# A transformer block on one core: attention products by groups of 512 queries, probabilities in contiguous blocks, one query buffer

## The chip, the core and the metric

The kernel runs on one core of a Trainium2 chip. The core has TensorE (matrix products, in profiles PE; its weight loads are PEld), VectorE (DVE), ScalarE (ACT), GpSimd (POOL) and SyncE (SP, which here only issues transfers). Each engine runs its own instructions in order and waits on semaphores. The metric is device time in microseconds (us) for one execution.

## What is computed

One layer: multi-head attention over 1024 tokens with 16 heads (128 plain and 64 rotary dimensions), a small side attention over tokens chosen by a gate, an output projection with residual and normalization, and a ternary-weight gated MLP with another normalization. The part that the change is about, from the reference:

```python
q = jnp.concatenate([q_nope, q_pe], axis=-1)
k = jnp.concatenate([k_nope, k_pe], axis=-1)
scores = jnp.einsum('bhqd,bhkd->bhqk', q, k) * scale
scores = jnp.where(causal[None, None], -jnp.inf, scores)
probs = jax.nn.softmax(scores.astype(jnp.float32), axis=-1).astype(q.dtype)
attn = jnp.einsum('bhqk,bhkd->bhqd', probs, v)
...
x = _layernorm(x + _L0_attn_ref(x, ...), axis=-1)
x = _layernorm(x + _L0_ffn_ref(x, ...), axis=-1)
```

## The kernel before

**Number format.** Nearly every operand of a product is kept as two parts, a high part (name ends in h) and a low part (l). ScalarE writes the high part as a copy, VectorE the low part as a subtraction (both by one helper line each, L1140 and L1298), and `three` (L838) makes three products: high by high, high by low, low by high.

**Tiles.** The 1024 queries of a head lie in 8 tiles of 128. For tile i: `qk` makes the scores against 128(i+1) keys on TensorE, into one of two buffers SC; VectorE masks them and finds the row extreme (L1367); ScalarE takes the exponential into Pb (`exp`, L1157); TensorE transposes Pb by 128x128 pieces (`tc`, L873), up to four into one of the ring's four buffers J0 to J3; ScalarE and VectorE bring them to PTh and PTl. Then `pv` multiplies the values Vh, Vl with PTh, PTl for a group of queries, the result goes to ATh, ATl, and `wo` multiplies it with the head's output weights and VectorE adds it to acc: a reciprocal (L1555) and two additions (L1563) per 256 queries.

**Groups before.** A `pv` group is 256 queries, two tiles; group g needs the keys of 2g+2 tiles, so a head has groups of 2, 4, 6 and 8 key tiles. PTh is `[128, 8 key tiles, 256]`, ATh has two buffers of 256. Each head parity has its own query buffer QNh, QNl, written in halves of 512 by `qn`.

**Order.** The order of everything is written out by hand in `head_steps`: a head has 8 slots, slot i begins with `qk` of tile i, then come two other steps, then `exp` of tile i (the place after which it comes is exp_at), then the rest. Each engine goes through this one list and runs its own part of each step, so a step that is placed later on TensorE is placed later on ScalarE and VectorE too. A ring step takes the next of J0 to J3 and waits until the step four places back in the ring has been read out. Steps next to the change: `kvn2` (four normalizations on ScalarE, L1252), `kt` (transposed keys), `ab` (head weights, which read Wqnh, Wqnl), `qp`, `kv`, `kpe` (projections for the next two heads), and, in the last two heads, `tern` (ternary weights), `rowadd`, `ln1` (row statistics, L1500 and L1504), `ln1n` (normalization, L1509), `ht` (transposes of the result for the MLP), `ug` (up and gate products of one of 32 MLP steps, 0 to 31), `m` (its activation) and `dn`.

**Passes.** Heads run in pairs, an even head and an odd one. The first pair is written out (FIRST), pairs 1 to 6 are a hardware loop (MID), the last pair is LAST, and EPILOGUE ends head 15 and runs the MLP.

## Time and profile before

| | |
|---|---|
| median of 3 runs | 686.48 us (684.96 to 688.63) |
| profiled execution | 685.76 us, its span 683.9 us |
| mean granted TensorE clock | 0.992 of full |
| TensorE busy | 645.7 us of the span |
| weight loads busy | 582.5 us |
| VectorE busy | 474.8 us |
| ScalarE busy | 400.3 us |
| GpSimd busy | 371.9 us |

Products are pipelined: each row of the timeline has the length of one product, but the next one starts long before it ends, so the distance between two starts says what it costs. Times in rows are counted from the start of the span. "idle before" is time in which the engine had nothing running, with what ended it.

### The profile page before, as it was taken

The numbers are of one execution on the slowest core, as the hardware profiler recorded it, in microseconds if no ns is written. First come the engines' busy times: TensorE is split into PE (matmuls) and PEld (weight loads), VectorE is DVE, ScalarE is ACT, GpSimd is POOL, SyncE is SP. The second block draws the span as 40 slices with busy tenths as digits, with TensorE's granted clock in tenths as the row PEclk, the third lists the DMA queues.
The fourth block names the chain that finished last, engine by engine and source line by source line (L and its number), as shares of the span: only waits on it lengthen the run. The fifth ranks groups of instructions, "written<-read, shape, count | busy, mean of one in ns | idle before, by whom it ended". The sixth has DMA issues, their size and how long they took to land.

```text
span 683.9 us, 14087 instructions
## 1 busy us (share of the span) xinstructions
PE 645.7 (94%) x4456; PEld 582.5 (85%) x4456; DVE 474.8 (69%) x1291; ACT 400.3 (59%) x934; POOL 371.9 (54%) x331
## 2 busy tenths in 40 slices
PE   8899989999999999999999999999999999889895
PEld 5788987898889988898889888988899888779895
DVE  4877367565766667666856586658666667897996
ACT  4884346744764475646664757456744767445552
POOL 7873368463844473456627472738454715431564
PEclk9999999999999999999999999999999999999998
DMA  7307142410451046103610342114510482000001
GB/s 233 115 2 176 41 93 50 114 56 16 109 132 54 0 99 154 54 0 92 146 46 23 92 101 60 54 46 92 115 54 0 108 240 75 10 1 1 1 17 47
DMA packets 23551, 49.85 MB, mean 73 GB/s; under 512 B 3168, under 2 KB 16352, under 8 KB 21600
## 3 DMA queue, kind: packets, MB, share of 16 engines
q1 hardware_dynamic: 22144, 47.82, 27.3%
q10 hardware_dynamic: 1376, 1.64, 0.7%
q8 instruction: 17, 0.28, 0.2%
q14 instruction: 14, 0.11, 0.1%
HBM read 16.94 MB, written 1.05 MB: 26 GB/s over the span
## 4 chain that ended last, share of the span: by engine, by line
PE 55%; DVE 14%; ACT 13%; issue 11%; POOL 4%; DMA 1%; DVEq 0%; ACTq 0%; POOLq 0%; SPq 0%
PE J L840 9%; PE J L842 9%; PE J L841 9%; PE J L873 4%; ACT Pb L1157 4%; DVE PTl L1298 4%; ACT kvraw L1252 3%; PE SC L860 3%; DVE SC L1367 3%; PE SC L862 3%; PE SC L861 3%; PE SC L864 3%; PE SC L863 3%; POOL rstd L711 3%; ACT PTh L1140 2%
## 5 line engine op out<-in xcount | busy, mean ns | idle before, releaser
L1298 DVE TENSOR_TENSOR PTl<-J,PTh 128x512 fp32r<-128x512 f32 (+1 forms) x192 | 102.8, 553 | 67.4 <-ACT PTh L1140 66.4
L1157 ACT ACTIVATE Pb<-SC,nm 128x128 f32<-128x128 f32 (+7 forms) x128 | 94.9, 741 | 54.8 <-DVE nm L1367 54.3
L1367 DVE CUSTOM_DVE_ANT_0 SC<-SC,mask 128x128 f32<-128x128 f32 (+7 forms) x128 | 97.1, 759 | 21.2 <-PE SC L864 20.0
L873 PE MATMUL J<-ident,Pb 128*128 128x128 f32 x576 | 88.9, 280 | 6.4 <-ACT Pb L1157 5.1
L840 PE MATMUL J<-PTh,Vh 128*128 128x256 f32 x320 | 88.7, 277 | 6.4 <-DVE PTl L1298 6.3
L1140 ACT ACTIVATE PTh<-J 128x512 fp32r<-128x512 f32 (+1 forms) x192 | 88.1, 492 | 8.3 <-PE J L873 7.6
L841 PE MATMUL J<-PTl,Vh 128*128 128x256 f32 x320 | 89.5, 280 | 0.0
L842 PE MATMUL J<-PTh,Vl 128*128 128x256 f32 x320 | 89.5, 280 | 0.0
L873 PEld LDWEIGHTS J<-ident,Pb 128*128 128x128 f32 x576 | 64.3, 141 | 15.4 <-ACT Pb L1157 6.8
L840 PEld LDWEIGHTS J<-PTh,Vh 128*128 128x128 f32 x320 | 60.2, 188 | 13.9 <-DVE PTl L1298 12.8
L860 PE MATMUL SC<-KNh,QNh 128*128 128x128 f32 (+2 forms) x192 | 69.3, 361 | 0.1
L1140 ACT ACTIVATE ATh<-J 128x256 fp32r<-128x256 f32 x64 | 24.5, 382 | 74.8 <-PE J L842 74.1
L862 PE MATMUL SC<-KNh,QNl 128*128 128x128 f32 (+2 forms) x192 | 66.0, 344 | 0.0
L863 PE MATMUL SC<-KK,QS 128*128 128x128 f32 (+2 forms) x192 | 66.0, 344 | 0.0
L861 PE MATMUL SC<-KNl,QNh 128*128 128x128 f32 (+2 forms) x192 | 65.9, 343 | 0.0
L864 PE MATMUL SC<-KK,QS 128*128 128x128 f32 (+2 forms) x192 | 65.9, 343 | 0.0
L1298 DVE TENSOR_TENSOR ATl<-J,ATh 128x256 fp32r<-128x256 f32 x64 | 27.0, 422 | 49.5 <-ACT ATh L1140 49.3
L841 PEld LDWEIGHTS J<-PTl,Vh 128*128 128x128 f32 x320 | 60.3, 188 | 0.4
L842 PEld LDWEIGHTS J<-PTh,Vl 128*128 128x128 f32 x320 | 60.5, 189 | 0.0
L1563 DVE SCALAR_TENSOR_TENSOR acc<-J,rs,acc 128x256 f32<-128x256 f32 x128 | 56.1, 480 | 2.7
L1252 ACT ACTIVATE kvraw<-kvraw,nmr,rstd 128x128 f32<-128x128 f32 x128 | 52.6, 486 | 2.5 <-POOL nmr L821 2.5
L1140 ACT ACTIVATE kvraw<-J 128x512 f32<-128x512 f32 x32 | 19.1, 598 | 58.1 <-PE J L842 58.1
(305 smaller groups left out, 1886.5 us busy)
## 6 DMA issues: line engine op xcount, KB each, us to landing
KK<-RK SPq DMA_DIRECT2D x30, 512.0 KB, 6.3
QS<-RQh SPq DMA_DIRECT2D x15, 256.0 KB, 7.5
QS<-RQl SPq DMA_DIRECT2D x15, 256.0 KB, 6.5
KX<-KX SPq DMA_DIRECT2D x14, 256.0 KB, 2.3
QX<-QX SPq DMA_DIRECT2D x14, 256.0 KB, 2.4
r_kv<-in_W_ckv SPq DMA_DIRECT2D x7, 384.0 KB, 3.5
r_o<-in_W_o SPq DMA_DIRECT2D x18, 128.0 KB, 2.1
r_qn<-in_W_qT SPq DMA_DIRECT2D x16, 128.0 KB, 2.1
```

Of the source, the lines that this page charges most:

```text
L840: mm(o, lhsT=wh, rhs=xh, start=start, stop=False)
L841: mm(o, lhsT=wh, rhs=xl, start=False, stop=False)
L842: return mm(o, lhsT=wl, rhs=xh, start=False, stop=stop)
L860: mm(o[:, k], lhsT=QNh[b][:, q], rhs=KNh[b][:, k], start=True, stop=False)
L861: mm(o[:, k], lhsT=QNh[b][:, q], rhs=KNl[b][:, k], start=False, stop=False)
L862: mm(o[:, k], lhsT=QNl[b][:, q], rhs=KNh[b][:, k], start=False, stop=False)
L863: mm(o[:, k], lhsT=QS[b][:, q], rhs=KD[b][:, k], start=False, stop=False)
L873: last = pe.transpose(o[:, tile(j - 4 * c)], Pb[i % 2][:, tile(j)], ident[:, :])
L1140: return act.activation(o, i, ACT.Copy)
L1157: act.activation(Pb[i % 2][:, w], SC[i % 2][:, s], ACT.Exp, bias=nm[:, i % 2:i % 2 + 1], scale=-1.0, accum_out=sm[:, b, i:i + 1]).then_inc ...
L1298: dve.tensor_tensor(o, i, h.bitcast(F32), ALU.subtract).then_inc(done[kind], 1)
L1367: dve.tensor_tensor_reduce(out=SC[i % 2][:, s], in0=SC[i % 2][:, s], in1=mask[:, 128 * (7 - i):S], scale=-SCALE, scalar=HIGH, op0=ALU.add, ...
```

## The change

Groups of 512 queries, two per head. Group g takes the key tiles below it (group 1: four, each with all 512 queries as one row), and four key tiles on its diagonal, with 512, 384, 256 and 128 queries. PTh and PTl become 29 blocks of 128 columns, laid out so that each of these rows is contiguous; `key_blocks` says to which blocks the transposes of a tile go. The blocks of group 0's diagonal lie where group 1's first keys lie. ATh and ATl are one buffer of 512 each. QNh and QNl are one buffer for all heads: half c is rewritten once tile 4c+3 of the head before has been scored. Wqnh and Wqnl move into a gap of PTh and PTl.

```diff
+DIAG = [0, 16]
+GAP = 26
+BLOCKS = 29
+def key_blocks(n):
+    i = TILE_OF[n]
+    g, ii, full = i // 4, i % 4, i >= 4 and n == CH0[i]
+    first, step, nb = (ii, 4, 4) if full else (DIAG[g] + ii, 3, ii + 1)
+    return slice(first, first + step * (nb - 1) + 1, step), nb
...
-        QNh.append(sb("QNh1", [128, S], F32R))
+        QNh.append(QNh[0])
...
-        PTh, PTl = sb("PTh", [128, T, 256], F32R), sb("PTl", [128, T, 256], F32R)
-        ATh = [sb(f"ATh{i}", [128, 256], F32R) for i in range(2)]
+        PTh, PTl = sb("PTh", [128, BLOCKS * 128], F32R), sb("PTl", [128, BLOCKS * 128], F32R)
+        ATh, ATl = sb("ATh", [128, 512], F32R), sb("ATl", [128, 512], F32R)
+        Wqnh, Wqnl = [X[:, 128 * GAP:128 * GAP + 256].rearrange("p (r n) -> p r n", r=2) for X in (PTh, PTl)]
...
+                add(6, True, ("ln1", 0, 0), ("ln1", 0, 1))
+                add(7, True, ("ln1n", 0, 0), *t(h, 6), ("ht", 0, 0), ("ln1n", 0, 1))
...
-            exp_at = [[2, 2, 2, 2, 2, 2, 2, 2], [2, 2, 2, 2, 2, 2, 2, 2]]
+            exp_at = [[2, 2, 2, 2, 2, 2, 2, 1], [2, 2, 2, 2, 2, 2, 2, 1]]
...
+                if i % 4 == 0 and not first:
+                    pe.wait_ge(done["qn"], count("qn", h, i // 4))
                 if i == 0 and not first:
-                    pe.wait_ge(done["qn"], count("qn", h, 1))
...
-                pe.wait_ge(pt_lo, NCH * h + CH0[2 * g + 2])
-                for j in range(2 * g + 2):
-                    q = slice(0, 256) if j <= 2 * g else slice(128, 256)
-                    last = three(o[:, q], Vh[b][:, j, :], Vl[b][:, j, :], PTh[:, j, q], PTl[:, j, q], j == 0, j == 2 * g + 1)
+                if g == 1:
+                    pe.wait_ge(pt_lo, NCH * h + CH0[7] + 1)
+                    for j in range(4):
+                        q = slice(512 * j, 512 * j + 512)
+                        three(o[:, :], Vh[b][:, j, :], Vl[b][:, j, :], PTh[:, q], PTl[:, q], j == 0, False)
+                pe.wait_ge(pt_lo, NCH * h + CH0[4 * g + 4])
+                for r in range(4):
+                    j, q = 4 * g + r, slice(128 * (DIAG[g] + 4 * r), 128 * (DIAG[g] + 3 * r + 4))
+                    last = three(o[:, 128 * r:], Vh[b][:, j, :], Vl[b][:, j, :], PTh[:, q], PTl[:, q], j == 0, r == 3)
...
-                    pe.wait_ge(done["pv"], count("pv", u, c))
+                    pe.wait_ge(done["pv"], count("pv", u, c // 2))
...
                     if kind == "qn":
+                        if not (isinstance(u, int) and u == 0):
+                            hold(act, sc_ready, T * (u - 1) + 4 * c + 4)
...
-                        wait(act, ready["wo"], 4 * u + c - 1)
-                        copy(ATh[c % 2][:, :], o[:, 0:256]).then_inc(hi["pv"], 1)
+                        wait(act, ready["wo"], 4 * u + 2 * c)
+                        copy(ATh[:, :], o[:, :]).then_inc(hi["pv"], 1)
```

The step lists change with it. In the loop, group 0 of a head stands in slot 5, right behind `qk` 5; group 1 stands in slot 1 of the next head. Steps wo 2 and wo 3 of a head are both in slot 2 of the next one. Steps wo 0 and wo 1 of the even head are in its slot 6; of the odd head, wo 0 is in slot 7 and wo 1 in slot 0 of the next head. The second half of `qn` is in slot 7, and `exp` of tile 7 comes after one step instead of two. In slot 2 of the even head the order is now tc of tile 1, kt 0, wo 2, kt 1, wo 3.

TensorE at the first product group of a head in the loop, before (J2 is a buffer of the ring, PTh and PTl the transposed probabilities, Vh0 and Vl0 the values of the even head), in the even head: the group of two key tiles, in slot 3.

```order
L840 MATMUL J2<-PTh,Vh0 128x256
L841 MATMUL J2<-PTl,Vh0 128x256
L842 MATMUL J2<-PTh,Vl0 128x256
L840 MATMUL J2<-PTh,Vh0 128x128
L841 MATMUL J2<-PTl,Vh0 128x128
L842 MATMUL J2<-PTh,Vl0 128x128
```

And after, the first group of the even head, in slot 5.

```order
L847 MATMUL J2<-PTh,Vh0 128x512
L848 MATMUL J2<-PTl,Vh0 128x512
L849 MATMUL J2<-PTh,Vl0 128x512
L847 MATMUL J2<-PTh,Vh0 128x384
L848 MATMUL J2<-PTl,Vh0 128x384
L849 MATMUL J2<-PTh,Vl0 128x384
L847 MATMUL J2<-PTh,Vh0 128x256
L848 MATMUL J2<-PTl,Vh0 128x256
L849 MATMUL J2<-PTh,Vl0 128x256
L847 MATMUL J2<-PTh,Vh0 128x128
L848 MATMUL J2<-PTl,Vh0 128x128
L849 MATMUL J2<-PTh,Vl0 128x128
```

Sixty products of a head, in four groups, become 36 in two.

VectorE in slots 6 and 7 of the last head, before: from the mask of tile 6 (128x896) to that of tile 7 (128x1024).

```order
L1367 ISA SC0,nm<-SC0,mask 128x896
L1367 ISA nm 128x1
L1298 TENSOR_TENSOR PTl<-J0,PTh 128x4x128
L1298 TENSOR_TENSOR PTl<-J1,PTh 128x2x128
L1555 RECIPROCAL rs<-sm 128x2
L1563 SCALAR_TENSOR_TENSOR acc<-J2,rs,acc 128x256 x2
L1517 TENSOR_TENSOR QS0<-J3,QNh0 128x256
L1517 TENSOR_TENSOR KK0<-J3,QNl0 128x256
L1500 BN_STATS st<-acc 128x6 x2
L1504 BN_AGGR mvl<-st 128x2 x2
L1367 ISA SC1,nm<-SC1,mask 128x1024
```

The same stretch after.

```order
L1380 ISA SC0,nm<-SC0,mask 128x896
L1380 ISA nm 128x1
L1311 TENSOR_TENSOR PTl<-J1,PTh 128x4x128
L1311 TENSOR_TENSOR PTl<-J2,PTh 128x2x128
L1566 RECIPROCAL rs<-sm 128x2
L1574 SCALAR_TENSOR_TENSOR acc<-J3,rs,acc 128x256 x2
L1566 RECIPROCAL rs<-sm 128x2
L1574 SCALAR_TENSOR_TENSOR acc<-J0,rs,acc 128x256 x2
L1511 BN_STATS st<-acc 128x6 x2
L1515 BN_AGGR mvl<-st 128x2 x2
L1511 BN_STATS st<-acc 128x6 x2
L1515 BN_AGGR mvl<-st 128x2 x2
```

The mask of tile 7 follows. A second wo and the first row statistics have come ahead of it; the low part of ht 0 has gone behind it.

TensorE between the transposes of tile 6 and of tile 7 in the last head, before, is filled by two up/gate steps of eight products each (the first of them shown) and a wo.

```order
L873 MATMUL J1<-ident,Pb0 128x128 x4
L873 MATMUL J2<-ident,Pb0 128x128 x3
L1053 MATMUL SC0<-QNh0,xTh 128x256
L1054 MATMUL SC0<-QS0,xTh 128x256
L1053 MATMUL SC0<-QNl0,xTh 128x256
```

After, only the transposes of ht 0 (L1030) lie between them, and the up/gate steps follow ht 1.

```order
L881 MATMUL J1<-ident,Pb0 128x128 x4
L881 MATMUL J2<-ident,Pb0 128x128 x3
L1030 MATMUL J3<-ident,acc 128x128 x4
L881 MATMUL J0<-ident,Pb1 128x128 x4
L881 MATMUL J1<-ident,Pb1 128x128 x4
L1030 MATMUL J2<-ident,acc 128x128 x4
L1066 MATMUL SC0<-QNh0,xTh 128x256
```

The last product group stands behind two of these up/gate steps; before, it stood behind four.

## Rows read from the trace of the kernel before

**Rows 1.** The page, part 1: busy us, share of the span, instructions.

```profile
PE 645.7 (94%) x4456; PEld 582.5 (85%) x4456; DVE 474.8 (69%) x1291; ACT 400.3 (59%) x934; POOL 371.9 (54%) x331
```

**Rows 2.** Busy time by stretch: stretch, its length, engines, clock, DMA.

```profile
core 0: us, PE busy (x) PEld busy (x) DVE busy (x) ACT busy (x) POOL busy (x), PEclk, DMA share, GB/s
200.00:280.00 80.00, 78.21 (x533) 70.40 (x534) 52.94 (x145) 50.35 (x120) 43.22 (x32) 1.00 0.27 66
600.00:683.90 83.90, 71.47 (x565) 68.81 (x564) 70.39 (x178) 40.99 (x100) 34.75 (x53) 0.97 0.04 14
```

**Rows 3.** Who TensorE waited for from 120 to 520: total, times, longest.

```profile
PE J L840 <- DVE PTl L1298: 3.1, 15, 0.3
PE J L873 <- ACT Pb L1157: 2.4, 11, 0.3
PE J L989 <- ACT kvraw L1252: 2.4, 5, 0.5
```

**Rows 4.** TensorE's timeline: start, length, line, tiles, shape.

```profile
300.65 0.28 PE L840 MATMUL J<-PTh,Vh 128*128 128x256 f32 x1
...
302.42 0.22 PE L840 MATMUL J<-PTh,Vh 128*128 128x128 f32 x1
...
302.71 0.95 PE L873 MATMUL J<-ident,Pb 128*128 128x128 f32 x7
...
318.31 0.34 PE L861 MATMUL SC<-KNl,QNh 128*128 128x384 f32 x1
...
318.84 0.33 PE L864 MATMUL SC<-KK,QS 128*128 128x384 f32 x1
...
329.08 0.39 PE L841 MATMUL J<-qcl,ABh 128*128 128x512 f32 x1
...
329.77 0.39 PE L1005 MATMUL J<-qcs,ABl 128*128 128x512 f32 x1
```

**Rows 5.** TensorE's timeline: waits in one pass, and the next pass's first.

```profile
304.44 1.09 PE L873 MATMUL J<-ident,Pb 128*128 128x128 f32 x8 [0.28 <-ACT Pb L1157]
...
317.67 0.63 PE L989 MATMUL J<-ident,kvraw 128*128 128x128 f32 x4 [0.47 <-ACT kvraw L1252]
...
376.87 0.33 PE L873 MATMUL J<-ident,Pb 128*128 128x128 f32 x1 [0.28 <-ACT Pb L1157]
```

**Rows 6.** Timeline of ScalarE and TensorE in slot 2 of an even head.

```profile
343.93 0.39 ACT L1140 ACTIVATE ATh<-J 128x256 fp32r<-128x256 f32 x1 [2.23 <-PE J L842]
...
344.82 1.65 ACT L1252 ACTIVATE kvraw<-kvraw,nmr,rstd 128x128 f32<-128x128 f32 x4
...
344.99 0.44 PE L873 MATMUL J<-ident,Pb 128*128 128x128 f32 x2 [0.17 <-ACT Pb L1157]
```

**Rows 7.** VectorE: two groups of the page's part 5, then one subtraction.

```profile
L1298 DVE TENSOR_TENSOR ATl<-J,ATh 128x256 fp32r<-128x256 f32 x64 | 27.0, 422 | 49.5 <-ACT ATh L1140 49.3
L1563 DVE SCALAR_TENSOR_TENSOR acc<-J,rs,acc 128x256 f32<-128x256 f32 x128 | 56.1, 480 | 2.7
...
620.99 0.69 DVE L1298 TENSOR_TENSOR PTl<-J,PTh 128x512 fp32r<-128x512 f32 x1 [0.25 <-ACT PTh L1140]
```

**Rows 8.** Timeline of the last head: VectorE's masks, statistics and normalization.

```profile
604.94 0.69 DVE L1367 CUSTOM_DVE_ANT_0 SC<-SC,mask 128x512 f32<-128x512 f32 x1
...
617.98 0.75 DVE L1500 BATCH_NORM_STATS2 st<-acc 128x6 f32<-128x256 f32 x2
...
618.92 1.23 DVE L1367 CUSTOM_DVE_ANT_0 SC<-SC,mask 128x1024 f32<-128x1024 f32 x1
...
622.94 0.73 DVE L1509 TENSOR_SCALAR acc<-acc,mvl,rsd 128x256 f32<-128x256 f32 x2
```

**Rows 9.** TensorE: the last product with V, and up/gate step 9.

```profile
628.96 0.27 PE L842 MATMUL J<-PTh,Vl 128*128 128x128 f32 x1
...
639.89 0.39 PE L1053 MATMUL SC<-QNh,xTh 128*128 128x256 f32 x1 [0.74 <-DVE CS L1462]
```

**Rows 10.** One stretch with its granted clock (columns as in rows 2).

```profile
570.00:575.00 5.00, 5.00 (x25) 4.83 (x24) 3.71 (x13) 3.50 (x8) 2.39 (x2) 0.67 0.50 171
```

More of the change, by code:

```diff
@@ L181, in attention_and_mlp @@
         Pb = [sb(f"Pb{i}", [128, S]) for i in range(2)]
-        PTh, PTl = sb("PTh", [128, T, 256], F32R), sb("PTl", [128, T, 256], F32R)
-        ATh = [sb(f"ATh{i}", [128, 256], F32R) for i in range(2)]
-        ATl = [sb(f"ATl{i}", [128, 256], F32R) for i in range(2)]
+        PTh, PTl = sb("PTh", [128, BLOCKS * 128], F32R), sb("PTl", [128, BLOCKS * 128], F32R)
+        ATh, ATl = sb("ATh", [128, 512], F32R), sb("ATl", [128, 512], F32R)
+        Wqnh, Wqnl = [X[:, 128 * GAP:128 * GAP + 256].rearrange("p (r n) -> p r n", r=2) for X in (PTh, PTl)]
         wip = KX[:, :, :]
@@ L289, in attention_and_mlp @@
         PER = {"xs": 4, "qc": T, "qm": 4, "kv": 4, "kpe": 2, "qp": 2, "qps": 2, "kt": 2, "ab": 1, "qn": 2,
-               "vs": 1, "pv": 4, "wo": 4, "side": 13, "tc": NCH, "wb": 1, "rwt": 1, "wtot": 3, "ht": 2}
+               "vs": 1, "pv": 2, "wo": 4, "side": 13, "tc": NCH, "wb": 1, "rwt": 1, "wtot": 3, "ht": 2}
         def count(kind, unit, c):
@@ L314, in attention_and_mlp @@
             ("qk", 0, 3), ("qn", 0, 1), ("rqrows", 0, 1), ("kt", 0, 1), ("exp", 0, 3), ("rkrows", 0, 0), ("rkrows", 0, 1),
[L315 removed]
+            ("ab", 1, 0), *t(0, 2), ("kvn2", 0, 2), ("vsh", 0, 1), ("wkv", 1, 0),
             ("qk", 0, 4), ("exp", 0, 4), ("top8", 0, 0), *t(0, 3), ("stk", 1, 0), ("stq", 1, 0), ("kvn2", 0, 3), ("vs", 1, 0),
[L317 to L318 removed]
+            ("qn", 1, 0), ("top8", 0, 1), ("kt", 1, 0), ("top8", 0, 2),
+            ("qk", 0, 5), ("pv", 0, 0), ("exp", 0, 5), ("top8", 0, 3), *t(0, 4), ("kt", 1, 1),
             ("qk", 0, 6), ("side", 0, 2), ("exp", 0, 6), *t(0, 5), ("wosp", 2, 0), ("wqn", 2, 0), ("wqp", 1, 0), ("kv", 1, 0),
             ("side", 0, 3), ("side", 0, 4), ("wo", 0, 0), ("wo", 0, 1),
[L321 removed]
+            ("qk", 0, 7), ("side", 0, 5), ("exp", 0, 7), ("kv", 1, 1), ("side", 0, 6), ("qn", 1, 1), ("kpe", 1, 0), ("kpe", 1, 1),
             ("ropek", 1, 0), *t(0, 6), ("side", 0, 7), ("kv", 1, 2), ("side", 0, 8), ("kv", 1, 3), ("side", 0, 9)]
@@ L418, in head_steps @@
                 add(4, first, ("io", 1, 0))
-                add(6, more, ("qn", n, 1))
                 add(4, more and not first, ("io", 1, 0))
-                add(6, True, *t(h, 5), ("wo", h, 1))
+                add(6, True, *t(h, 5))
+                add(6, last, ("wo", h, 0), ("wo", h, 1))
                 add(5, more, ("rw", n, 0))
                 add(6, more, ("skip", 0, 0))
-                add(7, more, ("wosp", h + 2, 0), ("wqn", h + 2, 0))
-                add(7, True, ("pv", h, 2), *t(h, 6))
+                add(7, more, ("wo", h, 0), ("qn", n, 1), ("wosp", h + 2, 0), ("wqn", h + 2, 0))
+                add(7, not last, *t(h, 6))
             if last:
@@ L470, in mlp_steps_of @@
             return a
-        EPILOGUE = [("wo", NH - 1, 2), *t(NH - 1, 7), one("ug", 2), one("ht", 1), one("m", 0), one("ug", 3), ("pv", NH - 1, 3),
-                    one("m", 1), one("ln1", 2), one("ug", 4), one("m", 2), ("wo", NH - 1, 3), one("ln1n", 2), one("ug", 5),
-                    one("m", 3), one("ln1", 3), one("ug", 6), one("m", 4), one("ln1n", 3)]
+        EPILOGUE = [*t(NH - 1, 7), one("ht", 1), one("ug", 0), one("ug", 1), one("m", 0), ("pv", NH - 1, 1), one("m", 1),
+                    one("ug", 2), one("ug", 3), ("wo", NH - 1, 2), one("m", 2), ("wo", NH - 1, 3), one("ug", 4), one("ln1", 2),
+                    one("m", 3), one("ug", 5), one("ln1n", 2), one("ln1", 3), one("ug", 6), one("m", 4), one("ln1n", 3)]
         for n in range(7, NM):
@@ L1023, in use @@
                 if kind == "wo":
-                    pe.wait_ge(done["pv"], count("pv", u, c))
+                    pe.wait_ge(done["pv"], count("pv", u, c // 2))
                     for t in range(2):
-                        last = three(o[:, 256 * t:256 * t + 256], ATh[c % 2][:, tile(t)], ATl[c % 2][:, tile(t)],
+                        q = tile(2 * (c % 2) + t)
+                        last = three(o[:, 256 * t:256 * t + 256], ATh[:, q], ATl[:, q],
                                      ABh[b][:, 256:512], ABl[b][:, 256:512], True, True)
@@ L1164, in run @@
                     if kind == "tc":
-                        i = TILE_OF[c]
-                        k = 4 * (c - CH0[i])
-                        nb = min(4, i + 1 - k)
-                        copy(PTh[:, k:k + nb, tile(i % 2)],
+                        blocks, nb = key_blocks(c)
+                        copy(PTh[:, :].rearrange("p (j q) -> p j q", q=128)[:, blocks, :],
                              o[:, 0:128 * nb].rearrange("p (j q) -> p j q", j=nb)).then_inc(hi["tc"], 1)
@@ L1370, in run @@
                     if kind == "tc":
-                        i = TILE_OF[c]
-                        k = 4 * (c - CH0[i])
-                        nb = min(4, i + 1 - k)
-                        dst = (slice(None), slice(k, k + nb), tile(i % 2))
-                        lo("tc", u, c, PTl[dst], o[:, 0:128 * nb].rearrange("p (j q) -> p j q", j=nb), PTh[dst])
+                        blocks, nb = key_blocks(c)
+                        h_, l_ = [X[:, :].rearrange("p (j q) -> p j q", q=128)[:, blocks, :] for X in (PTh, PTl)]
+                        lo("tc", u, c, l_, o[:, 0:128 * nb].rearrange("p (j q) -> p j q", j=nb), h_)
                     if kind == "xs":
```

42 lines of the change are left out of this document (16 added, 26 removed).

## The prediction

> **What bounds the kernel now.** I read the page's busy shares first. TensorE is busy 645.7 us of 683.9 [rows 1]. The stages then show where it is not: in the loop it is busy 78.2 of every 80 us, while VectorE has 53; from 600 us on TensorE has 71.5 of 83.9 and VectorE 70.4 [rows 2]. So the loop is bound by TensorE's own work, and the end is shared with VectorE. The waits in the loop agree: three kinds, 7.9 us in 400, none over 0.5 us [rows 3]. One pass (two heads) takes 376.87 - 304.44 = 72.43 us [rows 5]. Work taken from TensorE in the loop is time; a wait there is time too. In the last head and behind it, what counts is also when VectorE gets to an operation, for it runs in order.
>
> **The products with V.** What a product costs is the distance to the next start, not its length. From 300.65 to 302.42 lie 15 products of 256 columns: 0.118 us each. The three of 128 columns behind them take 0.29 together. The 512-wide rows lie 0.230 apart (0.69 for three), the 384-wide ones 0.177 [rows 4]. Before, a head has 48 products of 256 columns and four triples of 128: 48 x 0.118 + 4 x 0.29 = 6.82 us. After: 18 of 512, 6 of 384, 6 of 256 and two triples: 4.14 + 1.06 + 0.71 + 0.58 = 6.49. That is 0.33 a head, 5.3 us over 16 heads, of which 0.66 in a pass. The columns streamed are the same; only starts are saved. I take the measured distances for PTh too. Should the 512-wide ones lie 2 x 0.118 = 0.236 apart, the saving is 0. That is the lower bound.
>
> The page "TensorE: Matmul & The Clock Gate" of the Trainium skill (section "Wait — 56ns, not 53.3ns?") puts start-to-start at columns / 2.4 GHz plus about 2.5 ns. By it the 384 starts saved would be worth 384 x 2.5 ns = 0.96 us, an estimate from that page. The rows have 6 ns for two joined halves where that rule has 2.5, and the row decides.
>
> **Copies of the product.** The split of a group's result goes from 4 x 256 to 2 x 512 columns. VectorE's 256-wide subtraction is 422 ns, its 512-wide one 0.69 us [rows 7]: 4 x 0.42 - 2 x 0.69 = 0.3 us a head less there, and as little on ScalarE. VectorE has 27 us in 80 free in the loop [rows 2], so this is nothing there. The copy to the blocks has the same 128-element runs as before; only the stride between them changes: nothing.
>
> **Waits in the loop.** Three places move.
> First, the exponential of tile 7 now stands ahead of ScalarE's next copy instead of behind the copy of a product group. The wait at 304.44, 0.28 [rows 5], goes. But the new query copy (qn) sits behind it, its low part is needed before the ring's buffer is free, and the transposes of tile 7 wait for that some 0.4: even.
> Second, in slot 2 of the even head. The second group is 15 x 0.230 + 3 x 0.177 + 3 x 0.118 + 0.29 = 4.63 us instead of 21 x 0.118 + 0.29 = 2.77, its copy on ScalarE 0.2 longer than the 256-wide one, and the exponential of tile 1 stands behind it. So the wait at 344.99, 0.17, becomes 0.4. Behind that exponential stand four normalizations, 1.65 us [rows 6], then the copy of tile 1's transposes, which must be through before wo 3 gets buffer 1: another 0.25. Together +0.45.
> Third, in the odd head the wait of 0.47 at 317.67 [rows 5] for the same normalizations. Now TensorE has 1.8 us more of products ahead of it, so this place loses about 0.5.
> The sum is about 0; one run of transposes fewer between products gives 0.1, and rounding of the stretches another 0.05. So -0.83 a pass, -5.0 over six. Bounds: 0 (all new waits real, none of the old gone: +0.8 a pass) to -9 (all 1.4 us of waits gone by half).
>
> The single query buffer costs nothing: half 0 is written when tile 3 of the head before is long scored, half 1 behind qk 7 in TensorE's own order, and qk 4 of the next head asks for it four slots later. If that cover were gone, it would be one wait of about 1 us for copy and subtraction a head. The weights' place in PTh's gap is read by ab alone: nothing.
>
> **First pass.** Two heads save 0.66; the wo step that stood between the transposes and the side chain is gone, which can lengthen that wait: -0.5, between -0.7 and +1. **Head 14** (even head of the last pass): 0.33 saved; wo 0 now falls in slot 6, where VectorE also has the ternary weights, so the mask of tile 7 starts about 0.6 later and tile 7's transposes 0.4. I take 0, between -1 and +1.
>
> **The end, head 15.** Here the step lists were changed, and VectorE runs in order. Each wo costs it a reciprocal and two 480 ns additions [rows 7], 1.0 us.
> (a) The group of head 14 in slot 1 is 4.63 instead of 2.77 and begins 0.4 later: +2.2 where VectorE's long row (row additions, masks, ternary weights) waits behind it. (b) In slot 2 VectorE has two wo, not one: +1.0, and 0.2 for the wide subtraction. So the mask of tile 3, which starts at 604.94 now [rows 8], starts some 3.5 later. (c) TensorE then waits for exp 3 and does 0.8 more in slots 3 to 7, and in slot 6 VectorE does two wo and both row statistics (0.94 each, from 617.98 to 618.92) ahead of the mask of tile 7. That mask starts at 618.92 now [rows 8] and about 4.4 later then.
> (d) Now TensorE fills the wait for exp 7 with a group of 15 x 0.118 + 0.29 = 2.06 us, two up/gate steps and a wo, and the last group is over 10.2 us behind the start of that mask (628.96 + 0.12 - 618.92) [rows 8, 9]. After, the up/gate steps stand behind ht 1, and that behind: mask 1.15, normalization 0.65, two subtractions 1.1, low part of ht 0 0.75, normalization 0.65, with waits for ScalarE about 5.4 in all. Then ht 0.45, two up/gate steps 1.9 and the group 4.63: 12.4. So +2.3. (e) From that group's end to the wait of up/gate step 9 at 639.89 are 10.8 us [rows 9], VectorE's row; after, one more wo stands in it and fewer steps are done ahead: +1.3. From there on TensorE is bound as now, by the same work.
> (a) to (e): 4.4 + 2.3 + 1.3 = 8.0. Bounds: 3, if VectorE catches up in slots 3 to 6, where TensorE waits now too, and 11, if each wait in the row is as long as I reckon and the clock falls.
>
> **Sum**, against the profiled execution's 685.76 (its span 683.9 and 1.9 around it): -5.0 - 0.5 + 0 + 8.0 = +2.5, 688.3. The median of before is 0.7 above that execution, so the forecast for the median is 689.0. A measurement of this kernel tells about 0.5%, 3.4 us, from no change: 683.1 to 689.9 is "the same".
>
> **Rivals.**
> *The end is not VectorE's.* If the last mask starts no later than now, only the loop is left: -5.5, 681.0; if half of it comes true, 685. For it: TensorE waits in the last head now, and VectorE has 13 us free from 600 on [rows 2]. Against: those lie where it waits for the last products, not in the row between the masks. It decides from the point where the mask of tile 7 comes less than 2 us later. Chance 0.25.
> *The loop gains nothing.* The ring wait in slot 2 and the longer group ahead of exp 1 cost 0.8 a pass and not 0: 689.0 + 5.0 = 694.0. For it: the normalizations already end last at one place in each pass [rows 5]. Against: 0.45 of it is in the sum. Chance 0.15.
> *The clock falls in the end.* It is at 0.67 of full in 570 to 575 [rows 10], so for part of that stretch at 1.2 GHz; products then take twice as long and it costs up to (1 - 0.67) x 5 = 1.7 us. New idle before the up/gate steps could bring one more: 690.7. Chance 0.10.
> *Joining buys nothing*: the 512-wide rows of PTh cost two halves. 689.0 + 5.3 = 694.3. Chance 0.05. The page's 2.5 ns would come near to it, 693.3 as an estimate; the rows speak against both.
>
> **How the numbers follow.** The forecast's own case has 0.45, with a range of 686 to 692; two thirds of it lie within 0.5%. With the rivals' shares: faster by over 0.5% 0.22 (the first rival, less what of it lands inside), within 0.5% 0.38, slower 0.40. The range that leaves out no more than 2 in 10 goes from the first rival's 681 to the second's, 694.5.
>
> **What the profile after would show.** Products with V: 36 a head, 512-wide ones 0.230 apart, the group of eight tiles 4.63 us. A pass of 71.6. No wait of tile 7's transposes for exp over 0.3 in the even-to-odd change; a wait of 0.2 to 0.3 at wo 3 of the even head's slot 2. The last 128x1024 mask begins 4.4 later, reckoned from head 15's first score, and up/gate step 9 8.0 later. Wrong would be: a pass over 72.4 (the loop), or the last mask where it is now (the end).

## The result: slower by 1.1%

The changed kernel takes 694.33 us (median of 4 runs, 692.16 to 696.68), the kernel before 686.34 (4 runs, 684.96 to 688.63). The ratio is 1.0107 [1.0079, 1.0136]. The forecast was 689.0 with a range of 681.0 to 694.5: the sign is right, and the time lies 0.2 inside the range's upper end. The profiled execution took 693.23 us (its span is 691.4), where the forecast's sum has 688.3.

The changed kernel's page, its header line and part 1, answers to [rows 1]: 384 products fewer, and TensorE's busy time nearly the same.

```profile
span 691.4 us, 13249 instructions
...
PE 644.8 (93%) x4072; PEld 568.6 (82%) x4072; DVE 458.7 (66%) x1259; ACT 396.1 (57%) x902; POOL 371.6 (54%) x331
```

Where the time went is read from VectorE's masks of tile 0, one for each head, and of tile 7. These are the timeline rows of the changed kernel: heads 2, 14 and 15, then the last mask, and up/gate step 9 on TensorE.

```profile
122.76 0.29 DVE L1380 CUSTOM_DVE_ANT_0 SC<-SC,mask 128x128 f32<-128x128 f32 x1
...
549.58 0.29 DVE L1380 CUSTOM_DVE_ANT_0 SC<-SC,mask 128x128 f32<-128x128 f32 x1
...
586.97 0.29 DVE L1380 CUSTOM_DVE_ANT_0 SC<-SC,mask 128x128 f32<-128x128 f32 x1
...
619.54 1.23 DVE L1380 CUSTOM_DVE_ANT_0 SC<-SC,mask 128x1024 f32<-128x1024 f32 x1
...
647.44 0.39 PE L1066 MATMUL SC<-QNh,xTh 128*128 128x256 f32 x1 [0.69 <-DVE CS L1473]
```

The same three masks in the kernel before (its last mask and step 9 are in [rows 8, 9]).

```profile
122.66 0.29 DVE L1367 CUSTOM_DVE_ANT_0 SC<-SC,mask 128x128 f32<-128x128 f32 x1
...
556.61 0.29 DVE L1367 CUSTOM_DVE_ANT_0 SC<-SC,mask 128x128 f32<-128x128 f32 x1
...
592.65 0.29 DVE L1367 CUSTOM_DVE_ANT_0 SC<-SC,mask 128x128 f32<-128x128 f32 x1
```

| stretch | before | after | difference | forecast |
|---|---|---|---|---|
| start to the mask of head 2 | 122.66 | 122.76 | +0.1 | -0.5 |
| six passes of the loop | 433.95 | 426.82 | -7.1 | -5.0 |
| head 14 | 36.04 | 37.39 | +1.35 | 0 |
| head 15's first mask to its last | 26.27 | 32.57 | +6.3 | +4.4 |
| last mask to up/gate step 9 | 20.97 | 27.90 | +6.9 | +3.6 |
| from there to the end of the span | 44.0 | 44.0 | 0 | 0 |

So the loop gave more than forecast, and the last pair took much more. One caution on the borders: the group of a head that runs behind the next head's first mask is larger now, and one wo more runs behind that mask. By the columns of the timeline rows TensorE has 5,760 fewer of these two kinds to stream ahead of head 2's first mask than before, and as many more between head 15's first mask and step 9. That is a group of 4.67 us for one of 2.77, and a wo of 0.8: 2.7 us of work moved from the first line of the table to lines four and five.

The granted clock shows another part of it. Windows of 5 us in the changed kernel (columns as in [rows 2]; the last three are clock, DMA share, GB/s):

```profile
85.00:90.00 5.00, 3.49 (x13) 3.07 (x14) 4.33 (x25) 1.33 (x4) 4.70 (x3) 0.66 0.01 2
...
585.00:590.00 5.00, 4.28 (x15) 3.46 (x15) 4.90 (x14) 2.94 (x8) 0.13 (x1) 0.50 0.01 3
...
605.00:610.00 5.00, 5.00 (x21) 4.38 (x22) 3.12 (x6) 1.37 (x3) 0.01 (x1) 0.66 0.02 3
...
625.00:630.00 5.00, 4.80 (x24) 4.71 (x25) 2.97 (x7) 2.49 (x5) 0.00 (x0) 0.60 0.00 0
```

By windows of 2.5 us the last three stretches had about 6.8, 3.4 and 6.8 us at the lower level, some of it beyond the edges of these windows. Ahead of each of the four stands one long wait of TensorE. Its timeline:

```profile
86.51 0.35 PE L936 MATMUL J<-mean,QX 64*64 64x8 f32 x2 [2.07 <-DVEq L1361]
...
584.26 0.75 PE L881 MATMUL J<-ident,Pb 128*128 128x128 f32 x4 [3.19 <-ACT Pb L1170]
...
604.98 0.77 PE L881 MATMUL J<-ident,Pb 128*128 128x128 f32 x3 [2.89 <-ACT Pb L1170]
...
621.57 0.63 PE L1030 MATMUL J<-ident,acc 128*128 128x128 f32 x4 [3.02 <-DVE acc L1520]
```

These are the side attention in the first pass, the transposes of tile 7 of head 14, those of tile 3 of head 15, and the first transposes for the MLP. Before, the first was 1.41, the second 0.88 and the third 1.61 long. Both kernels have a low stretch between 32 and 40 us and one in the last 7 us of the span; between these the kernel before fell once, at 570 to 575 [rows 10]. The profile shows one execution of each, but the mean granted clock is known for every one: 0.975 to 0.982 in the four of the changed kernel, 0.984 to 0.998 in those of the kernel before that were timed beside the experiments.

### The profile page after: what moved, and what is told of

It reads as the page before. It is cut to its first block, busy times and chain, and to the rows that moved or that the text cites. A ratio compares the mean times of both kernels' runs of the same rounds, so it can differ in the third digit from the quotient of the medians.

```text
span 691.4 us, 13249 instructions
## 1 busy us (share of the span) xinstructions
PE 644.8 (93%) x4072; PEld 568.6 (82%) x4072; DVE 458.7 (66%) x1259; ACT 396.1 (57%) x902; POOL 371.6 (54%) x331
## 4 chain that ended last, share of the span: by engine, by line
PE 63%; ACT 16%; DVE 11%; issue 7%; DMA 1%; POOL 1%; ACTq 0%; POOLq 0%; DVEq 0%; SPq 0%
PE J L847 11%; PE J L849 10%; PE J L848 10%; PE J L881 5%; ACT kvraw L1263 5%; ACT Pb L1170 4%; PE SC L868 3%; PE SC L871 3%; PE SC L870 3%; PE SC L869 3%; PE SC L872 3%; PE SC L1066 2%; PE SC L1067 2%; ACT PTh L1153 2%; DVE PTl L1311 2%
## 5 line engine op out<-in xcount | busy, mean ns | idle before, releaser
L881 PE MATMUL J<-ident,Pb 128*128 128x128 f32 x576 | 91.2, 282 | 14.6 <-ACT Pb L1170 9.9
L881 PEld LDWEIGHTS J<-ident,Pb 128*128 128x128 f32 x576 | 66.8, 143 | 28.3 <-DVE QNl L1311 7.2
L1311 DVE TENSOR_TENSOR ATl<-J,ATh 128x512 fp32r<-128x512 f32 x32 | 22.1, 691 | 82.2 <-ACT ATh L1153 82.0
L1153 ACT ACTIVATE ATh<-J 128x512 fp32r<-128x512 f32 x32 | 19.1, 598 | 96.7 <-PE J L849 96.7
L849 PE MATMUL J<-PTh,Vl 128*128 128x512 f32 x192 | 67.3, 350 | 0.0
L848 PE MATMUL J<-PTl,Vh 128*128 128x512 f32 x192 | 67.2, 350 | 0.0
L847 PE MATMUL J<-PTh,Vh 128*128 128x512 f32 x192 | 66.6, 347 | 0.2 <-DVE PTl L1311 0.2
L653 POOL TENSOR_TENSOR KX<-KX,CS 128x1024 f32<-128x1024 f32 x7 | 16.8, 2404 | 57.3 <-DMA KX<-KX 57.3
L748 POOL CAST Vh<-kvraw 128x1024 fp32r<-128x1024 f32 x15 | 15.8, 1055 | 51.5 <-ACT kvraw L1263 51.5
L847 PEld LDWEIGHTS J<-PTh,Vh 128*128 128x128 f32 x192 | 36.8, 191 | 5.6 <-DVE PTl L1311 0.5
```

What stands on the lines that cost most here:

```text
L847: mm(o, lhsT=wh, rhs=xh, start=start, stop=False)
L848: mm(o, lhsT=wh, rhs=xl, start=False, stop=False)
L849: return mm(o, lhsT=wl, rhs=xh, start=False, stop=stop)
L881: last = pe.transpose(o[:, tile(j - 4 * c)], Pb[i % 2][:, tile(j)], ident[:, :])
L1153: return act.activation(o, i, ACT.Copy)
L1311: dve.tensor_tensor(o, i, h.bitcast(F32), ALU.subtract).then_inc(done[kind], 1)
```

## The experiments

Each ratio below is to the kernel before, timed beside it on the same chip. What the rows show is one execution of each kernel.

### The clock: fill the waits

`fill_last` puts products that nobody reads ahead of the three waits in the last pass.

```diff
+            def fill(o, n):
+                for _ in range(n):
+                    mm(o[:, :], lhsT=mask[:, 0:128], rhs=mask[:, 128:640], start=True, stop=True)
...
+                if isinstance(h, int) and (h, n) == (NH - 2, CH0[7]):
+                    fill(o, 13)
+                if isinstance(h, int) and (h, n) == (NH - 1, CH0[3]):
+                    fill(o, 12)
                 if c == 0:
                     pe.wait_ge(exp_done, T * h + i + 1)
...
                 if kind == "ht":
+                    if c == 0:
+                        fill(o, 12)
                     pe.wait_ge(ln_done, c + 1)
```

> The changed kernel, with 13, 12 and 12 products of 512 columns that nobody reads put on TensorE ahead of its three long waits of the last pass (3.19 us before the transposes of tile 7 of head 14, 2.89 before those of tile 3 of head 15, 3.02 before the first transposes for the MLP). Nothing else moves, and each batch is shorter than its wait. Theory (each long wait is followed by some 3.4 us at half clock, which costs up to 1.7 us): the granted clock stays at 1.00 behind all three, and the kernel gets 3 x 1.5 = 4.5 us faster, 689.8, ratio to the kernel before 1.004. Rival (the end is late for VectorE's row alone, and products slowed there stand beside other waits): the clock stays up and the time moves by less than 1 us, ratio 1.010.

Ratio 1.0051 [1.0032, 1.0070], by the ratios 3.8 us better than the changed kernel, and the mean granted clock of its six executions was 0.985 to 0.992. Two falls were gone; the first had only come later, at 0.74 in 590 to 595, where the group still ran 6.16 us (592.68 to 598.84) instead of 4.66.

`fill_more` adds 8 to the first pass (`c == 10` of `side`, ahead of its `side_dve` wait), 3 to `wtot` and 4 to head 14's second group.

> The kernel of the first filling run, with unread products of 512 columns at three more places: 8 ahead of the wait of 2.07 us for the side attention in the first pass, 3 ahead of the wait for the weights' sum at the start of head 15, and 4 ahead of head 14's second product group, which still ran at half clock there (6.16 us instead of 4.66). Theory (the clock is the price of those waits): both falls go, 1.5 us each, ratio to the kernel before 1.0005 to 1.002 instead of 1.005. Rival (the falls stand where VectorE sets the time): ratio 1.005 as before.

Ratio 1.0072 [1.0053, 1.0092]. The last pass had no fall at all:

```profile
588.00:593.00 5.00, 4.15 (x25) 2.43 (x24) 3.85 (x10) 4.58 (x11) 2.05 (x2) 1.00 0.00 2
...
606.00:611.00 5.00, 4.79 (x27) 3.02 (x26) 4.68 (x10) 2.15 (x5) 1.56 (x1) 1.00 0.00 0
...
625.00:630.00 5.00, 3.30 (x27) 3.03 (x27) 4.18 (x10) 3.69 (x8) 0.00 (x0) 1.00 0.01 3
```

Its masks stand at 592.12 and 621.72 and up/gate step 9 at 647.91: 29.60 and 26.19 us for the stretches that take 32.57 and 27.90 in the changed kernel. The falls therefore cost 3.0 and 1.7 us there, 4.7 in all for three, in these two executions. What is left over the kernel before, 3.3 + 5.2 = 8.5, is not the clock's. In the first pass the filling stood in the wrong place: an earlier wait in the same step came first (2.14, ahead of the eight products), so they followed it and made that stretch longer. From the start of head 0's first mask to head 2's it took 92.97 us, against 91.24 in `fill_last`, with a fall at 90 to 95 in both. `rows_first` (below) has the same eight products and had no fall there: 91.26. So the products cost about 1.7, and a fall there costs as much.

### The order in the last pair

`cover14` moves head 14's wo 1 behind the scores of tile 7.

```diff
-                add(6, True, *t(h, 5), ("wo", h, 0), ("wo", h, 1))
+                add(6, True, *t(h, 5), ("wo", h, 0))
+                add(6, more, ("wo", h, 1))
+                add(7, last, ("wo", h, 1))
```

> The changed kernel, with wo 1 of head 14 moved from its slot 6 to slot 7, behind the scores of tile 7. Theory (the product group that left this place had covered the wait for exp 7): 0.8 us of products come into the gap and the mask of tile 7 starts 1.0 earlier on VectorE, so the wait of 3.19 shrinks to about 1.4, and if it takes the fall of the clock along, another 1.5 is won behind it: head 15 starts 1.8 to 3.3 earlier, the kernel 691 to 692.5. Rival (head 15's own VectorE row sets the end wherever it starts): head 15's masks of tile 3 and 7 stay where they are, no change, 694.

Ratio 1.0112 [1.0092, 1.0132], no change of the time, as the rival has it. Head 14 became 1.0 shorter, and the wait 2.46 and not 1.4, now for the additions of that very wo, which hold the ring's buffer:

```profile
586.82 0.44 PE L883 MATMUL J<-ident,Pb 128*128 128x128 f32 x2 [2.46 <-DVE acc L1576]
```

The last mask came 33.25 behind head 15's first, 0.7 more than before the edit.

`late15` gives head 15 nearly the old order.

```diff
-                add(6, True, ("ln1", 0, 0), ("ln1", 0, 1))
-                add(7, True, ("ln1n", 0, 0), *t(h, 6), ("ht", 0, 0), ("ln1n", 0, 1))
+                add(6, True, ("ln1", 0, 0))
+                add(7, True, ("ln1n", 0, 0), *t(h, 6), ("wo", h, 1), ("ht", 0, 0), ("ln1", 0, 1))
+                add(7, True, ("ug", 0, 0), ("ug", 0, 1), ("ln1n", 0, 1))
...
-                add(6, last, ("wo", h, 0), ("wo", h, 1))
+                add(6, last, ("wo", h, 0))
...
-        EPILOGUE = [*t(NH - 1, 7), one("ht", 1), one("ug", 0), one("ug", 1), one("m", 0), ("pv", NH - 1, 1), one("m", 1),
+        EPILOGUE = [*t(NH - 1, 7), one("ug", 2), one("ht", 1), one("m", 0), one("ug", 3), ("pv", NH - 1, 1), one("m", 1),
...
```

> The changed kernel with the end of head 15 in nearly the order of the kernel before: wo 1 and the second row statistics behind the scores of tile 7, and up/gate steps 0 and 1 ahead of its transposes, step 2 behind them. Theory of the prediction (two wo and both row statistics ahead of the last mask cost VectorE 1.9 us, and the steps behind ht 1 leave TensorE idle): the last mask starts 1.9 earlier, up/gate step 9 comes 2 to 4 earlier, and without the wait of 3.0 one fall of the clock less: 689 to 692. Rival (the group of 4.6 us at the end cannot be hidden, whatever the order): less than 1 us, 693.5 to 694.

Ratio 1.0157 [1.0137, 1.0178]: a miss. The last mask came 1.1 earlier (31.48 behind the first) and not 1.9, and then TensorE waited elsewhere, for the transposed rows' low part, which had got behind the wo and the statistics:

```profile
625.86 0.58 PE L1067 MATMUL SC<-QNh,xTh 128*128 128x256 f32 x1 [3.17 <-DVE KK L1529]
```

`rows_first` (on top of `fill_more`) puts the row sum, two row additions and a ternary step ahead of head 14's second group.

```diff
-                add(1, last, ("rwt", 0, 0))
...
-                    add(1, True, ("rowadd", 0, 0), ("rowadd", 0, 1), ("tern", 0, 8))
+                    slots[1][0:0] = [("rwt", 0, 0), ("rowadd", 0, 0), ("rowadd", 0, 1), ("tern", 0, 8)]
```

> As the run with the six fillings, and in head 15 the row sum, the first two row additions and a ternary step stand ahead of head 14's second product group instead of behind it. In the changed kernel VectorE has nothing to do for 4.9 us beside that group and then 2.5 us of these steps. Theory (the wide group holds VectorE's row up, +2.2 in the prediction): the mask of tile 3 starts 1.5 to 2.5 earlier, and the end 1 to 2.5, ratio 0.003 below that of the run with the six fillings. Rival (TensorE's group is only put off by that row): no change or slower.

Ratio 1.0113 [1.0088, 1.0137]: a miss too. The group was put off by a new wait of 2.02 for the row, a fall of the clock came behind it, and the last mask stood 31.99 behind the first instead of 29.60. None of the three orders tried mended the last pair.

`hybrid` keeps the changed first pair and loop and gives the last two heads the old groups of 256, the old layout inside the same buffers, and the old order.

```diff
+        def narrow(h):
+            return isinstance(h, int) and h >= NH - 2
...
+                if narrow(h):
+                    pe.wait_ge(pt_lo, NCH * h + CH0[2 * g + 2])
+                    for j in range(2 * g + 2):
+                        z = 0 if j <= 2 * g else 128
+                        q = slice(256 * j + z, 256 * j + 256)
+                        last = three(o[:, z:256], Vh[b][:, j, :], Vl[b][:, j, :], PTh[:, q], PTl[:, q], j == 0, j == 2 * g + 1)
+                    return last
...
```

> The changed kernel's first pair and loop, with the last two heads as in the kernel before: product groups of 256 queries, their probabilities in the old layout inside the same buffers, and the old order of head 15 and of the steps behind it. Only the single query buffer stays there. Theory (all that the change loses, it loses in the last pair: the order and the wide groups there, and three falls of the clock behind the waits that they make): the loop's gain of 7.1 us stays whole, the last two heads take what they took, one fall of the clock instead of three: 679 to 681, ratio 0.989 to 0.992. Rival (the loop hands the last pair a start that costs it the same, or the clock falls anyway): ratio 0.998 to 1.005.

Ratio 0.9931 [0.9915, 0.9947]: faster than the kernel before. The loop's six passes took 426.69. Head 15 and the rest took what they took before: masks at 590.00 and 616.27 and step 9 at 637.25, so 26.27 and 20.98. In this execution the clock stayed up there, with waits no longer than 1.62:

```profile
570.00:600.00 30.00, 26.12 (x176) 23.00 (x175) 26.73 (x73) 15.84 (x38) 16.77 (x11) 1.00 0.03 10
600.00:640.00 40.00, 35.55 (x272) 33.62 (x271) 34.88 (x89) 20.65 (x49) 10.69 (x17) 1.00 0.00 1
```

It fell a little short of the forecast 0.989 to 0.992. Two stretches of the rows account for it: head 14 took 37.40 where the kernel before took 36.04, for it begins with head 13's group of 4.67 and then has its own old ones, and head 0's first mask to head 2's took 92.43 where it took 90.96 before, with a fall in it. `hybrid_first` moves one wo into that wait.

```diff
-            ("side", 0, 3), ("side", 0, 4), ("wo", 0, 0), ("wo", 0, 1),
+            ("side", 0, 3), ("side", 0, 4), ("wo", 0, 0),
...
-            add(0, b == 0, ("wo", m, 1))
+            add(0, b == 0 or first, ("wo", m, 1))
```

> The kernel with the changed loop and the old last pair, and in the first pass wo 1 of head 0 moved from its slot 6 to slot 0 of head 1, between the transposes of tile 7 and the side attention, where the kernel before had a wo and the change left nothing. Theory (the wait of 2.07 us there, against 1.41 before, is what lets the clock fall at 85 to 95 in the changed kernel and in each of its variants): the wait goes to 1.3 or less, the clock stays at 1.00 there, the first pass gets 1 to 2 us shorter, ratio to the kernel before 0.990 to 0.9915. Rival (the fall comes anyway, or the first pass is bound by its weights' transfers): ratio 0.993 as without it.

Ratio 0.9904 [0.9876, 0.9932], the fastest kernel of the study: 680.70 us where the kernel before took 688.00. Its wait and two windows:

```profile
87.49 0.25 PE L967 MATMUL J<-mean,QX 64*64 64x8 f32 x2 [1.38 <-DVEq L1394]
...
85.00:90.00 5.00, 3.47 (x23) 2.89 (x22) 4.13 (x13) 1.82 (x6) 4.73 (x3) 1.00 0.00 0
90.00:95.00 5.00, 5.00 (x28) 4.17 (x26) 2.40 (x22) 1.22 (x4) 4.84 (x5) 1.00 0.13 28
```

From head 0's first mask to head 2's it took 89.32 us, the least of all kernels (90.96 before). The steps of `hybrid` took 92.43 there in its own execution and 90.98 in the changed kernel's, for the low stretch was 6.9 us long in the one and 3.4 in the other; so about 1.7 of the 3.1 between the two new kernels may be the edit's. That the shorter wait is what kept the clock up is not shown. In this place the clock fell in most kernels with the wait of 2.07, but not in `split_row`, which waits 2.10 there, and it fell in `before_oneq`, which waits 1.41. The whole kernel's gain over `hybrid` is 0.3%, and the two intervals overlap.

Its last pair shows something else. The steps there are those of `hybrid`, yet in this execution the clock fell in head 15 (0.72 in 590 to 595, behind waits of 1.12 and 1.49 that `hybrid` has too), and head 15's first mask to its last took 27.78 instead of 26.27. The same happened in `before_row`, a kernel with the old order (below): 0.66 in 595 to 600, and again 27.78. So one fall costs 1.5 us there, and the old order does not always keep the clock up.

### What the loop gained

A pass of the kernel before takes 72.47 us from the second on (71.63 the first), one of the changed kernel 71.14. The rows of VectorE and GpSimd in the kernel before show something that the prediction had not looked at:

```profile
473.23 2.39 POOL L743 TENSOR_TENSOR Vl<-kvraw,Vh 128x1024 fp32r<-128x1024 f32 x1
...
473.44 2.47 DVE L1541 SCALAR_TENSOR_TENSOR row<-r_o,iocol,row 128x256 f32<-128x256 f32 x1
```

And in the changed kernel:

```profile
470.19 0.48 DVE L1552 SCALAR_TENSOR_TENSOR row<-r_o,iocol,row 128x256 f32<-128x256 f32 x1
...
470.31 2.61 POOL L750 TENSOR_TENSOR Vl<-kvraw,Vh 128x1024 fp32r<-128x1024 f32 x1
```

The same VectorE instruction takes 2.47 us where GpSimd's subtraction began 0.21 before it, and 0.48 where that began 0.12 behind it. In the first case it ends 0.29 behind GpSimd's. Its place in the step list is the old one: the change's other edits moved it in time. The page "SBUF — State Buffer" of the Trainium skill (section "SBUF: two separate sides") says that VectorE and GpSimd share one pair of ports, which a VectorE instruction with two SBUF inputs and a GpSimd instruction that reads SBUF hold against each other for the whole instruction, whichever starts first. This trace agrees, with 2.47 against 0.48, and GpSimd's own instruction is the longer one (2.61 for 2.39) where VectorE's began first.

`before_row` moves only that instruction in the kernel before.

```diff
-                add(6, True, *t(h, 5), ("wo", h, 1))
-                add(5, more, ("rw", n, 0))
+                add(6, True, *t(h, 5))
+                add(6, more, ("rw", n, 0))
+                add(6, True, ("wo", h, 1))
```

> The kernel before with one step moved: VectorE's weight-row product (line 1541, row<-r_o,iocol,row) of the odd head goes from slot 5 to slot 6, behind the transposes' low parts. In the kernel before it takes 2.5 us in the loop's passes from the second on, against 0.48 in the even heads: it starts 0.2 after GpSimd's subtraction Vl<-kvraw,Vh and ends 0.3 after it. Theory (VectorE stands still beside GpSimd there, and the mask of tile 6 and the product group of tile 7 come 0.87 later in each such pass): it takes 0.5, a pass gets 0.85 shorter, and the kernel 4 to 5 us faster, 682.5, ratio 0.9935. Rival (TensorE catches up elsewhere, and the pass is 72.4 for its own work): ratio 0.999 to 1.001.

Ratio 0.9961 [0.9945, 0.9977]. The instruction took 0.47 in the loop and a pass 71.92: 0.55 gained, not 0.85. Why not more is not shown: TensorE has no new wait, and those of a pass went from 1.5 to 1.3.

`after_row` moves it in the changed kernel into the subtraction.

```diff
-                add(5, more, ("rw", n, 0))
+                add(5, more and first, ("rw", n, 0))
+                if more and not first:
+                    slots[6].insert(0, ("rw", n, 0))
...
```

> The changed kernel with the same step moved into GpSimd's subtraction: in the loop's odd head it goes from the end of slot 5, where it starts 0.12 before that subtraction and takes 0.48, behind the mask of tile 6, where the subtraction has 1.5 us to go. Theory (part of the change's gain in the loop is that the two missed each other): it takes about 1.8, the low parts behind it come 1.8 later, and a pass gets 0.4 to 1.0 longer, 2.5 to 6 us in all: 697 to 700. Rival: VectorE has slack there, no change, 694.

Ratio 1.0126 [1.0102, 1.0149], an interval that overlaps the changed kernel's: a miss. It took 1.22 there instead of 1.8, for it began 1.45 behind the subtraction's start, with 0.94 of it to go, and a pass took 71.26, 0.1 more: nothing here. In every collision of the loop's later passes looked at, it ends 0.28 or 0.29 behind the subtraction. That a collision costs only where VectorE has no slack behind it fits both runs, but is argued.

`split` cuts the wide products again, all but the first row of each group.

```diff
-                        q = slice(512 * j, 512 * j + 512)
-                        three(o[:, :], Vh[b][:, j, :], Vl[b][:, j, :], PTh[:, q], PTl[:, q], j == 0, False)
+                        for z, w in ((0, 512),) if j == 0 else ((0, 256), (256, 256)):
+                            q = slice(512 * j + z, 512 * j + z + w)
+                            three(o[:, z:z + w], Vh[b][:, j, :], Vl[b][:, j, :], PTh[:, q], PTl[:, q], j == 0, False)
...
+                    for z0, z1 in ((0, 512),) if j == 0 or r > 1 else ((0, 256), (256, 512)):
```

> The changed kernel, with the 512-wide and 384-wide products with V cut into two (the first row of each group stays whole): 54 products a head instead of 36, the same columns. If joining is what pays (0.33 us a head for 24 products less, by the prediction's sum), 18 more cost 0.2 to 0.26 a head, a pass 0.4 to 0.5 longer, the kernel 3 to 4 us slower, 697 to 698. If a start costs only the 2.5 ns of the Trainium skill's page TensorE: Matmul & The Clock Gate: 18 x 2.5 ns = 0.045 a head, 0.7 us in all, an estimate from that page. If the loop's gain comes from waits that went, no more than 1 us either.

Ratio 1.0262 [1.0245, 1.0279]: far more than any of the three. A pass took 72.88. The groups of a pass took 13.90 against 13.18, so 0.72 of the 1.74; of the rest the instruction above was the greater part, for it had got into the subtraction again (2.64, begun 0.03 behind it). `split_row` moves it past.

```diff
-                add(5, more, ("rw", n, 0))
+                add(6, more, ("rw", n, 0))
```

> The changed kernel with its products cut again, as in the run with 54 products a head, and the weight-row product of the odd head moved behind the transposes' low parts in slot 6, past GpSimd's subtraction. In the run without that move it took 2.65 us in the loop's later passes, a pass 72.9 us, of which 0.7 are the product groups themselves. Theory (the other 1.0 was that collision): it takes 0.5, a pass 71.9 to 72.2, the kernel 4 to 6 us faster than the cut one, ratio 1.018 to 1.020 to the kernel before. Rival (the cut products cost it elsewhere): 72.9 as before, ratio 1.026.

Ratio 1.0227 [1.0209, 1.0245]. The instruction took 0.48 and a pass 71.91, as the theory has it; the whole kernel gained 2.4 us by the ratios and not 4 to 6.

`before_oneq` gives the kernel before the single query buffer, with the places of `qn` that it asks for in every head, and nothing else. The cut shows the even head's.

```diff
-        QNh.append(sb("QNh1", [128, S], F32R))
+        QNh.append(QNh[0])
...
-                add(5, True, ("pv", h, 1), *t(h, 4), ("qn", n, 1))
+                add(5, True, ("pv", h, 1), *t(h, 4))
...
-                add(7, True, ("pv", h, 2), *t(h, 6))
+                add(7, True, ("pv", h, 2), ("qn", n, 1), *t(h, 6))
...
```

> The kernel before with one query buffer for all heads: the second half of qn goes to slot 7, behind the scores of tile 7 and the third product group, and the scores of tile 4 wait for it. Theory of the prediction (the buffer costs nothing, since TensorE's own order covers it): ratio 0.998 to 1.002, apart from the weight-row product, which may miss GpSimd in the new order and give back 0.55 a pass. Rival (the copy and low part of qn in slot 7 stand ahead of the transposes' in the ring): a wait of 0.4 at one place of each head, +5 to 6 us, ratio 1.008.

Ratio 0.9955 [0.9938, 0.9972]: neither. It is faster, though the weight-row product still took 2.44 to 2.49 from the second pass on. A pass took 71.58, 0.9 less. The new place of `qn` in slot 7, behind the third group, gives the exponential of tile 7 time: the wait of 0.28 for it [rows 5] is gone from the trace. The other 0.6 has no one row; buffer and place moved together, and no run tells them apart.

## Why the prediction was right and where it was wrong

**Sign and mechanism: right in the main.** The loop gains and the last pair loses more. `hybrid` shows that: with the old last pair the same loop is 0.7% faster than the kernel before. That the last pair loses it to VectorE's row is argued from the late last mask, and no run isolates it: the three that moved VectorE's steps (`cover14`, `late15`, `rows_first`) gained nothing.

**The range held by some luck.** Its upper end, 694.5, was the price of a loop that gains nothing, and the loop gained 7.1. What filled that room is the clock, which the forecast's own case left out, and the measured 694.33 was 0.2 inside.

**The products.** The forecast had 6.49 us a head; an even head takes 1.87 + 4.67 = 6.54. A 512-wide start costs 0.2327, not the 0.230 of one pair of rows (408.45 to 411.94 for fifteen):

```profile
408.45 0.40 PE L847 MATMUL J<-PTh,Vh 128*128 128x512 f32 x1
...
411.94 0.34 PE L847 MATMUL J<-PTh,Vh 128*128 128x384 f32 x1
...
412.47 0.28 PE L847 MATMUL J<-PTh,Vh 128*128 128x256 f32 x1
```

Two joined halves are so worth 0.236 - 0.2327 = 3 ns, and not the 6 ns that the forecast read. The page "TensorE: Matmul & The Clock Gate" of the Trainium skill (section "Wait — 56ns, not 53.3ns?") has about 2.5 ns for a product's fixed cost, and this trace comes close to it with its 3 ns. What pays is that rows of 128 columns go: a triple of 384 takes 0.53, the two triples of 256 and 128 that it replaces 0.64 (`split`, 459.98 to 460.62). The rival "joining buys nothing" was thus nearly right about the halves and wrong about the time. Its price was a slip in the sum: with 0.236 for a 512-wide product the forecast's own terms give 4.25 + 1.06 + 0.71 + 0.58 = 6.60 a head, which still saves 0.22, 3.6 us over 16 heads, and not 0. So the lower bound of this term and the 694.3 (and the 693.3 beside it) were wrong: by that rival's condition the sum gives 690.7.

**Waits in the loop.** Of the places named, three came out: the transposes of tile 7 wait 0.40 for qn's low part (forecast 0.4), those of tile 1 wait 0.39 (0.4), and the old 0.28 went. The wait for the normalizations fell from 0.47 to 0.24 and not to 0, and wo 3 in slot 2 shows no wait. But a pass is 71.14 and not 71.6, and the six together gain 2.1 more than forecast. The rows of one pass (from 339.24 before, from 336.18 after) say where the 1.33 a pass come from. The product groups, each to the start of what follows it, take 13.93 before (6.81 in the even head, 7.12 in the odd one) and 13.18 after: 0.75, where the forecast has 0.66. TensorE's waits are 1.5 before and 1.0 after: 0.5, where the forecast has "The sum is about 0". That is the step that failed. It priced the waits from the places that move and left out what VectorE did in the kernel before: `before_row` gains 0.55 a pass by taking the collision away, and `before_oneq` 0.9 by the place of `qn`. The two overlap with each other and with the groups (0.75 + 0.55 + 0.9 is 2.2, not 1.33), so they don't add up, and how much of the 0.5 is which was not measured.

**The single buffer.** "Costs nothing" held; that its new order would be a gain (`before_oneq`, ratio 0.9955) was not seen.

**Head 14: "I take 0".** It was +1.35. The mask of tile 7 did come 0.75 later (forecast 0.6), and the transposes as much (0.4). But head 14's third group had stood ahead of these transposes and TensorE had waited 0.88 only; now it waits 3.19 with nothing ahead, 2.3 more, and the clock falls. Beside kernels whose clock stayed up there (35.1 in `before_oneq` and `before_row`, 37.37 in `fill_more`) the loss is 2.3 as well. The forecast priced VectorE's delay and not the cover that left TensorE.

**Head 15, (a) to (e): 8.0.** Without the clock the two stretches lost 3.3 + 5.2 = 8.5 (`fill_more`). The size is right by its sum, and partly so by errors that cancel: (a) to (c) were 1.1 too high and (d) and (e) 1.6 too low.

**The clock: a rival at 0.10, one fall of 1.7.** It happened three times there, for 4.7 us, on top of the forecast's own case and not in its place. With the better loop (-2.1), first pair and head 14 (+2.0) and (a) to (e) (+0.5) that makes 5.1, and the miss, 693.23 against 688.3, is 4.9. The prediction saw "new idle" and took one fall as unlikely, though its own step (d) gave TensorE a wait of over 2 us.

**First pass.** The longer wait at the side chain was named and priced up to +1: it is 2.07 for 1.41, with a fall behind it in this execution, and the stretch came to +0.1. The term was mis-sized by more than that shows. With the 2.7 us of work that moved behind the border (see the table), TensorE had that much less to do up to head 2's first mask; the forecast counted the group's 1.9 at the end, in (a), and took only 0.66 off here. From head 0's first mask to head 2's TensorE's waits are 7.3 before and 9.9 after, so 2.6 more: it gained nothing because its waits grew by as much.

**The other rivals.** "The end is not VectorE's" fell: the last mask came 6.3 later. "The loop gains nothing" fell at 71.14.

## What to carry to other kernels

When work is taken from a place or joined into a larger piece, ask what wait it had covered there. In the last pair that cover was worth 2.3 us in head 14 alone, and behind TensorE's waits of about 3 us slower products cost another 1.6 each on average. A schedule tuned for one grain is worth keeping where the engines are near balance: new groups in the TensorE-bound loop and old ones in the last pair gave 0.7% (1.0% with one more wo moved) where the change alone lost 1.1%. When a time is split at a border, count the work on either side of it too. And look for one VectorE instruction that takes five times its usual time in some passes: where a gain can't be summed from the edits, such a collision may have moved.
